# A flamingo block on one core: where bulk transfers, statistics and GpSimd's pieces stand in the attention loop

## The chip, the core and the metric

One core of a Trainium2 chip runs the whole program. The metric is the device time of one execution in microseconds. The engines are TensorE (PE, with its weight loads PEld), VectorE (DVE), ScalarE (ACT), GpSimd (POOL) and SyncE (SP), which here only issues transfers. Each engine runs its own program in order; they meet in semaphores.

## What is computed

`x` is 8 x 224 x 2048, the context 8 x 750 x 512, all float32. Cut to what matters:

```python
def attention(q, k, v, mask):          # 32 heads of 64, 8 groups of keys and values, context of 750
    scores = jnp.einsum('bsgrd,btgd->bgrst', xq, xk) / math.sqrt(64) + mask
    probs = jax.nn.softmax(scores, axis=-1)
    return jnp.einsum('bgrst,btgd->bsgrd', probs, xv)

x = x + jnp.tanh(g_xattn[0]) * attention(_layernorm(x), ctx, ctx, mask)
x = x + jnp.tanh(g_ffn[0]) * ffn(_layernorm(x), ...)    # router, top 8 of 512 slots, gate
```

## The kernel before

The first phase, the attention, lasts to about 935 us; the second, the feed-forward part, follows and is not touched. A group is one batch and one of its 8 groups of keys and values: 64 groups. Two groups make a double group (`both`, 0 to 31), four double groups a batch; `at` is `both % 4`. The 224 rows of a batch are 128 top rows (`xa`) and 96 rest rows (`xb`, three buffers), and a group has 4 + 3 = 7 units of 128 rows by 750 scores. A double group is worked off in 7 steps (`p` = 0 to 6) of two units each.

All engines loop over the steps, each with its own lead. In step i TensorE transposes the exponentials of the pair i + 1, computes the scores of the pair i + 3, and adds the value products: of pair i - 1 with the low half of the exponentials (`value_low`), of pair i with the high half (`value_high`). VectorE takes the maxima of the scores (i + 3) and adds finished groups to x (`add_part`). ScalarE takes the exponentials (i + 2, line 753) and copies the transposed ones out of PSUM (i + 1, line 749). GpSimd computes the low bfloat16 half of the copied exponentials of pair i + 1 (line 588), the main piece of its step; the exponentials have four buffers, two pairs. Beside it GpSimd splits the keys (`split_k`, line 548) and the values (`split_v`, line 553) of each group, a sixteenth of W1 in two steps of the double groups 2 to 9 (line 615), and computes the factors of the layer norm of the next batch (`root`, `factors`).

SyncE's queue is written out by hand. Keys and values have two buffers each, so a load waits until the group two before is done: `scored` counts units whose scores are computed, `valued` units whose values are added. Also on this queue: `load_top` (1 MB of x), `load_rest` (768 KB), `gather_rest` and `spread_rest` (four small transfers each, which bring the statistics of rest rows from four blocks of partitions together and back), and `spill_rest` (twelve transfers of 64 KB, which store a batch's finished rest rows).

The statistics of the next batches are computed by VectorE one piece at a time:

```python
                if p == 3:
                    for window in (2 * both, 2 * both + 1):
                        next_stats(window)
```

With `window + 5` over 8 giving batch and place, the three rest pieces of batch b + 2 stand in step 3 of the double groups at = 1 (one) and at = 2 (two), the four top pieces in those at = 3 and at = 0.

## Time and profile before

| | |
|---|---|
| median of 3 runs | 1233.67 us (1232.75 to 1234.44) |
| the profiled execution, own time | 1235.78 us |
| its span, first to last instruction | 1233.9 us |
| TensorE busy | 1094.9 us (89%) |
| ScalarE busy | 891.0 us (72%) |
| GpSimd busy | 865.7 us (70%) |
| VectorE busy | 863.5 us (70%) |
| granted TensorE clock, mean | 0.957 of 2.4 GHz |
| moved by DMA | 95.56 MB |

Busy shares are averages over both phases. A row of a timeline stands for one or several equal instructions; "idle" in brackets is the time in which the engine had nothing to do before it, and the arrow names what ended it. A granted clock of 1.00 is 2.4 GHz, 0.50 is 1.2 GHz.

### The profile page before, as it was taken

Reading aid. Unit: us, or ns where it says so; the run is one execution under the profiler, and the core shown is the slowest. Engines: PE = TensorE matmul, PEld = TensorE weight load, DVE = VectorE, ACT = ScalarE, POOL = GpSimd, SP = SyncE. Lnnn points to the kernel's source line nnn. Section 1 sums busy time; section 2 is a strip of 40 time slices with the busy share of each in tenths; the row PEclk is TensorE's granted clock in tenths of the full one; section 3 lists DMA queues with packets and bytes.
Section 4 is the critical chain, followed back from the end, with each engine's and each line's share of the span. In section 5 each row is a group of like instructions: output and inputs, shape, how many; then the busy total and the mean of one; then the engine's idle time right before and its main releaser. Section 6 shows DMA issues by size and latency. Waiting matters only on the chain.

```text
span 1233.9 us, 42837 instructions
## 1 busy us (share of the span) xinstructions
PE 1094.9 (89%) x18276; PEld 790.3 (64%) x18276; DVE 863.5 (70%) x2134; ACT 891.0 (72%) x1159; POOL 865.7 (70%) x600
## 2 busy tenths in 40 slices
PE   4878977897789878968987999989998999999998
PEld 3666766675667656746765777767775755555554
DVE  5667756785578567747775777777884499767676
ACT  3778966896689669957976898999993244465545
POOL 5779977997799679787967988998994021242333
PEclk9889988998899889988997999999998999999999
DMA  9422232123213322321142123123114700002124
GB/s 318 135 53 56 51 89 65 41 59 80 65 42 65 87 65 47 92 74 40 41 100 65 41 57 69 42 51 73 48 40 142 284 37 1 1 34 92 81 103 171
DMA packets 102588, 95.56 MB, mean 77 GB/s; under 512 B 84481, under 2 KB 85505, under 8 KB 98562
## 3 DMA queue, kind: packets, MB, share of 16 engines
q1 hardware_dynamic: 101682, 91.79, 26.5%
q8 instruction: 146, 2.39, 0.8%
q10 hardware_dynamic: 720, 1.05, 0.2%
q14 instruction: 40, 0.33, 0.1%
HBM read 71.75 MB, written 20.97 MB: 75 GB/s over the span
## 4 chain that ended last, share of the span: by engine, by line
PE 54%; POOL 14%; ACT 13%; issue 10%; DVE 4%; DMA 3%; SPq 2%; POOLq 0%; DVEq 0%; ACTq 0%
PE psum L950 11%; PE psum L1006 11%; POOL arena L588 10%; PE psum L937 9%; ACT arena L749 6%; PE psum L982 5%; ACT arena L753 4%; PE psum L970 4%; PE psum L971 4%; PE psum L1092 3%; DMA arena<-in_x_rest 2%; DVE arena L1355 2%; POOL arena L548 2%; PE psum L993 2%; PE psum L917 1%
## 5 line engine op out<-in xcount | busy, mean ns | idle before, releaser
L588 POOL TENSOR_TENSOR arena<-arena 128x1536 bf16<-128x1536 f32 x224 | 613.6, 2748 | 87.8 <-ACT arena L749 87.4
L1355 DVE CUSTOM_DVE_ANT_0 arena<-psum,arena 128x750 f32<-128x750 f32 x448 | 406.9, 937 | 192.2 <-PE psum L937 152.6
L749 ACT ACTIVATE arena<-psum 128x768 f32<-128x768 f32 x448 | 362.7, 810 | 137.8 <-PE psum L950 74.7
L753 ACT ACTIVATE arena<-arena,neg_max 128x750 f32<-128x750 f32 x448 | 409.6, 914 | 30.8 <-DVE neg_max L1355 30.8
L937 PE MATMUL psum<-arena 64*128 64x512 bf16 (+1 forms) x2688 | 271.5, 335 | 65.3 <-DVE neg_max L1355 42.2
L950 PE MATMUL psum<-ident,arena 64*128 64x64 f32 x5376 | 270.4, 234 | 53.0 <-ACT arena L749 50.6
L950 PEld LDWEIGHTS psum<-ident,arena 64*128 64x128 f32 x5376 | 215.9, 142 | 124.9 <-issue 115.5
L937 PEld LDWEIGHTS psum<-arena 64*128 64x128 bf16 x2688 | 127.2, 97 | 161.1 <-issue 57.1
L971 PE MATMUL psum<-arena 128*128 128x64 bf16 (+1 forms) x2688 | 201.6, 195 | 1.4 <-issue 1.4
L970 PE MATMUL psum<-arena 128*128 128x65 bf16 (+1 forms) x2688 | 202.6, 197 | 0.0
L971 PEld LDWEIGHTS psum<-arena 128*128 128x128 bf16 (+1 forms) x2688 | 180.6, 100 | 1.6 <-issue 1.6
L970 PEld LDWEIGHTS psum<-arena 128*128 128x128 bf16 (+1 forms) x2688 | 181.2, 99 | 0.1
L1006 PE MATMUL psum<-arena 128*128 128x512 bf16 x672 | 162.1, 385 | 0.0
L982 PE MATMUL psum<-arena 128*128 128x65 bf16 (+1 forms) x2688 | 131.9, 199 | 0.0
L548 POOL TENSOR_TENSOR arena<-arena 128x750 bf16<-128x750 f32 x64 | 92.0, 1437 | 49.4 <-DMA arena<-in_k_t 49.4
L1006 PEld LDWEIGHTS psum<-arena 128*128 128x128 bf16 x672 | 63.3, 97 | 78.7 <-issue 1.9
L982 PEld LDWEIGHTS psum<-arena 128*128 128x128 bf16 (+1 forms) x2688 | 103.3, 100 | 15.9
L736 ACT ACTIVATE arena<-psum 128x512 bf16<-128x512 f32 x56 | 33.0, 591 | 107.0 <-PE psum L993 107.0
L1290 DVE SCALAR_TENSOR_TENSOR arena<-psum,r_den,arena 128x64 f32<-128x64 f32 x448 | 97.3, 277 | 2.3
L565 POOL TENSOR_TENSOR ga<-mv_all,eps_col 128x1 f32<-128x1 f32 (+1 forms) x12 | 2.3, 190 | 97.2 <-DVE mv_all L1310 97.2
L634 POOL TENSOR_TENSOR arena<-arena 128x512 bf16<-128x512 f32 x9 | 9.4, 1040 | 82.6 <-issue 61.9
L1248 DVE CAST arena<-psum 128x512 bf16<-128x512 f32 (+1 forms) x62 | 38.7, 624 | 28.8 <-PE psum L917 28.8
(167 smaller groups left out, 1085.9 us busy)
## 6 DMA issues: line engine op xcount, KB each, us to landing
arena<-in_k_t SPq DMA_DIRECT2D x128, 187.5 KB, 3.3
arena<-in_v_rows SPq DMA_DIRECT2D x64, 192.0 KB, 3.5
out<-arena SPq DMA_DIRECT2D x10, 1024.0 KB, 3.9
arena<-in_x_top SPq DMA_DIRECT2D x8, 1024.0 KB, 6.8
arena<-in_x_rest SPq DMA_DIRECT2D x8, 768.0 KB, 4.9
spill<-arena SPq DMA_DIRECT2D x96, 64.0 KB, 2.2
arena<-spill SPq DMA_DIRECT2D x6, 1024.0 KB, 10.3
arena<-in_w_t SPq DMA_DIRECT2D x4, 1024.0 KB, 16.6
```

The lines of the kernel that those rows point to most:

```text
L548: pool.tensor_tensor(k_lo[:, g % 2, :], k_raw[:, g % 2, :], high(k_raw[:, g % 2, :]), ALU.subtract).then_inc(k_split, 1)
L588: pool.tensor_tensor(p_lo[:, slots, :], p_sb[:, slots, :], high(p_sb[:, slots, :]), ALU.subtract).then_inc(p_split, 1)
L749: act.activation(p_sb[:, n % RING, :].rearrange("p (c h q) -> p h c q", h=2, q=HALF), turned_ps, ACT.Copy).then_inc(evac_a, 1)
L753: act.activation(s_sb[:, n % RING, 0:CTX], s_sb[:, n % RING, 0:CTX], ACT.Exp, bias=neg_max[:, n % 4, :], scale=-1.0).then_inc(exped, 1)
L937: mm = pe.matmul(flat_ps[:, score_at(s) + cols.start:score_at(s) + cols.stop], q[rows, both % 2, p, :], kk, start=(term == 0), stop=(term ...
L950: mm = pe.transpose(psum[:, 4 + h, c * HALF:(c + 1) * HALF], s_sb[rows, n % RING, c * 128:(c + 1) * 128], ident[rows, rows])
L970: pe.matmul(o, hi, high(v_raw[0:rows, u, c, :]), start=(fresh and c == 0), stop=False, skip_group_check=True)
L971: pe.matmul(o[:, 0:D], hi, v_lo[0:rows, u, c, :], start=False, stop=False, skip_group_check=True)
L982: mm = pe.matmul(mix_ps[:, g % 2, at:at + D + 1], lo, high(v_raw[0:rows, g % 2, c, :]), start=False, stop=(c == NCH - 1), skip_group_check ...
L1006: mm = pe.matmul(psum[:, 2, :], h[:, j, kk, :], w, start=(k == 0 and n == 0), stop=(k == KC - 1 and n == 2))
L1290: ins = dve.scalar_tensor_tensor(xs, o[:, m, 0:D], r_den[:, m:m + 1], xs, ALU.mult, ALU.add)
L1355: dve.tensor_tensor_reduce(s_sb[:, n % RING, 0:CTX], flat_ps[:, score_at(s):score_at(s) + CTX], mask_sb[:, max(m - REP + 1, 0), :], -1.0, ...
```

## The change

Five things are moved; no computation is added or removed.

- SyncE, in each double group: the odd keys `load_k(2 * both + 3)` and the even values `load_v(2 * both + 2)` now stand ahead of spill, gather, `load_top` and `load_rest`. `load_top` moves from at = 0 to at = 1, `load_rest` and `spread_rest` from at = 1 to at = 2.
- VectorE: the rest statistics stand in steps 1 and 3 of at = 3, the top statistics in step 3 of at = 0 and at = 1 of the batch after; the merge of the rest statistics in step 6 instead of 3. The early statistics of the second phase stand in steps 1 and 5 instead of 3.
- GpSimd: `split_v` of the odd group moves from step 1 to 0, `root` from 0 to 2, `factors` from 1 to 3, the W1 (and Wq) pieces from 0 and 3 to 2 and 6.
- ScalarE: `norm_top` moves from step 4 to 6, the second `norm_rest` from step 0 to 1.

```diff
--- before.py
+++ after.py
@@ -442,24 +442,23 @@
                 if both > 0:
                     sp.wait_ge(valued, 2 * UNITS * both)
                     load_v(2 * both + 1)
+                if at == 2 and b + 1 < BATCH:
+                    spread_rest(b + 1)
+                if both + 1 < PAIRS:
+                    sp.wait_ge(scored, 2 * UNITS * (both + 1))
+                    load_k(2 * both + 3)
+                    sp.wait_ge(valued, 2 * UNITS * both + UNITS)
+                    load_v(2 * both + 2)
                 if at == 0 and b > 0:
                     spill_rest(b - 1)
                 if at == 0 and b + 1 < BATCH:
                     gather_rest(b + 1)
-                if at == 0 and b + 2 < BATCH:
+                if at == 1 and b + 2 < BATCH:
                     load_top(b + 2)
-                if both + 1 < PAIRS:
-                    sp.wait_ge(scored, 2 * UNITS * (both + 1))
-                    load_k(2 * both + 3)
-                if at == 1 and b + 1 < BATCH:
-                    spread_rest(b + 1)
-                if at == 1 and b + 2 < BATCH:
+                if at == 2 and b + 2 < BATCH:
                     if b >= 1:
                         sp.wait_ge(spilled[(b + 2) % 3], 16 * REP * NB * ((b - 1) // 3 + 1))
                     load_rest(b + 2)
-                if both + 1 < PAIRS:
-                    sp.wait_ge(valued, 2 * UNITS * both + UNITS)
-                    load_v(2 * both + 2)
 
             def load_piece(i):
                 slot = i % STAGE_SLOTS
@@ -595,7 +594,7 @@
                                        ALU.mult, ALU.add).then_inc(top_second, 1)
                 if both < 0:
                     continue
-                if p == 1:
+                if p == 0:
                     split_v(2 * both + 1)
                 if both + 1 < PAIRS:
                     if p == 1:
@@ -605,18 +604,18 @@
                     if p == 5:
                         split_v(2 * both + 2)
                 if both % 4 == 2 and both // 4 + 1 < BATCH:
-                    if p == 0:
+                    if p == 2:
                         root(both // 4 + 2, whole)
-                    if p == 1:
+                    if p == 3:
                         factors(both // 4 + 2, whole)
-                if p in (0, 3) and 2 <= both < 2 + KC // 2:
-                    n = 2 * (both - 2) + p // 3
+                if p in (2, 6) and 2 <= both < 2 + KC // 2:
+                    n = 2 * (both - 2) + p // 6
                     pool.wait_ge(w1_loaded[n // 4], 16)
                     pool.tensor_tensor(w1_lo[:, n, :], w1_raw[:, n, :], high(w1_raw[:, n, :]), ALU.subtract).then_inc(w1_split, 1)
                 if both == PAIRS - 1 and p == 5:
                     root2(0, EARLY)
-                if p in (0, 3) and both == 10:
-                    n = p // 3
+                if p in (2, 6) and both == 10:
+                    n = p // 6
                     pool.wait_ge(wq_hi_done, 1)
                     pool.tensor_tensor(wq_cat[:, 8 * n:8 * n + 8, BOT:2 * BOT], wq_raw[:, 8 * n:8 * n + 8, :], wq_cat[:, 8 * n:8 * n + 8, 0:BOT],
                                        ALU.subtract).then_inc(wq_split, 1)
@@ -765,14 +764,14 @@
                         exp_unit(2 * (i + 2) + s)
                 if i in (-2, -1):
                     round_first(i + 3)
-                if both >= 0 and p == 4 and both + 2 < PAIRS:
+                if both >= 0 and p == 6 and both + 2 < PAIRS:
                     norm_top(both + 2)
                 later = both // 4 + 1
                 if both >= 0 and both % 4 == 3 and later < BATCH:
                     if p == 0:
                         norm_rest(later, 0)
+                    if p == 1:
                         norm_rest(later, 1)
-                    if p == 1:
                         norm_rest(later, 2)
                 if both == 1 and p == 0:
                     act.wait_ge(small_loaded, 80)
@@ -1318,13 +1317,20 @@
                 dve.tensor_scalar(h_rows[:, j % 2, :], rows[:, 512 * j:512 * j + 512], mv_all[:, t, 0:1], rstd_all[:, t:t + 1],
                                   ALU.subtract, ALU.mult).then_inc(h_staged, 1)
 
-            def next_stats(window):
-                b, at = divmod(window + 5, KV)
-                b += 1
-                if window >= 3 and b < BATCH and at < NB:
-                    rest_stats(b, at)
-                elif window >= 3 and b < BATCH and at < NB + 4:
-                    top_stats(b, at - NB)
+            def next_stats(both, p):
+
+                if both == 0:
+                    for j in {0: (0, 1), 1: (2,)}.get(p, ()):
+                        rest_stats(1, j)
+                    for c in {3: (0, 1), 5: (2, 3)}.get(p, ()):
+                        top_stats(1, c)
+                b = (both - 3) // 4 + 2
+                if both < 3 or b >= BATCH:
+                    return
+                for j in {(3, 1): (0,), (3, 3): (1, 2)}.get((both % 4, p), ()):
+                    rest_stats(b, j)
+                for c in {(0, 3): (0, 1), (1, 3): (2, 3)}.get((both % 4, p), ()):
+                    top_stats(b, c)
 
             def early_stats(window):
                 u, c = divmod(window - EARLY_AT, 4)
@@ -1372,19 +1378,15 @@
                         split_q(both + 1, 0)
                     if p == 6:
                         split_q(both + 1, 1)
-                if both == 0:
-                    for j in {0: (0, 1), 1: (2,)}.get(p, ()):
-                        rest_stats(1, j)
-                    for c in {3: (0, 1), 5: (2, 3)}.get(p, ()):
-                        top_stats(1, c)
-                if p == 3 and both % 4 == 1 and both // 4 + 1 < BATCH:
-                    merge_top(both // 4 + 1)
-                    merge_rest(both // 4 + 1)
-                if p == 3:
-                    for window in (2 * both, 2 * both + 1):
-                        next_stats(window)
-                        if EARLY_AT <= window < EARLY_AT + 4 * EARLY:
-                            early_stats(window)
+                next_stats(both, p)
+                if both % 4 == 1 and both // 4 + 1 < BATCH:
+                    if p == 3:
+                        merge_top(both // 4 + 1)
+                    if p == 6:
+                        merge_rest(both // 4 + 1)
+                window = 2 * both + p // 5
+                if p in (1, 5) and EARLY_AT <= window < EARLY_AT + 4 * EARLY:
+                    early_stats(window)
                 if i == NP - 4:
                     stage_h(0, 0)
                     stage_h(0, 1)
```

On SyncE, the double groups at = 0 and at = 1 of batch 1 (both = 4 and 5) before. It begins behind the first keys and values of double group 4; `in_k_t` is a load of keys, `in_v_rows` of values:

```order
L416 DMA spill<-arena 256x1x64 x12
L404 DMA gathered<-stats_rest 32x3x6 x4
L392 DMA arena<-in_x_top 128x2048
L396 DMA arena<-in_k_t 64x750 x2
L399 DMA arena<-in_v_rows 128x6x64
L396 DMA arena<-in_k_t 64x750 x2
L399 DMA arena<-in_v_rows 128x6x64
L396 DMA arena<-in_k_t 64x750 x2
L409 DMA ln_mv<-mv_rest 32x6 x4
L389 DMA arena<-in_x_rest 128x1536
L399 DMA arena<-in_v_rows 128x6x64
```

The same engine of the changed kernel, the same batch's second to fourth place: it begins with the gathers, which follow the twelve spills at the end of a double group at = 0.

```order
L404 DMA gathered<-stats_rest 32x3x6 x4
L396 DMA arena<-in_k_t 64x750 x2
L399 DMA arena<-in_v_rows 128x6x64
L396 DMA arena<-in_k_t 64x750 x2
L399 DMA arena<-in_v_rows 128x6x64
L392 DMA arena<-in_x_top 128x2048
L396 DMA arena<-in_k_t 64x750 x2
L399 DMA arena<-in_v_rows 128x6x64
L409 DMA ln_mv<-mv_rest 32x6 x4
L396 DMA arena<-in_k_t 64x750 x2
L399 DMA arena<-in_v_rows 128x6x64
L389 DMA arena<-in_x_rest 128x1536
```

The bulk (`in_x_top`, `in_x_rest`, spill and gather) stands behind the keys and values of its double group, the spread (`ln_mv`) and `in_x_rest` one double group later.

On GpSimd, one double group with W1 pieces before, from its step 6 of the one ahead (line 588 the main piece of a step, 615 the W1 piece, 553 a value split, 548 a key split):

```order
L588 TENSOR_TENSOR arena<-arena 128x1536 x2
L615 TENSOR_TENSOR arena<-arena 128x512
L588 TENSOR_TENSOR arena<-arena 128x1536
L553 TENSOR_TENSOR arena<-arena 128x384
L548 TENSOR_TENSOR arena<-arena 128x750
L588 TENSOR_TENSOR arena<-arena 128x1536 x2
L615 TENSOR_TENSOR arena<-arena 128x512
L588 TENSOR_TENSOR arena<-arena 128x1536
L548 TENSOR_TENSOR arena<-arena 128x750
L588 TENSOR_TENSOR arena<-arena 128x1536
L553 TENSOR_TENSOR arena<-arena 128x384
L588 TENSOR_TENSOR arena<-arena 128x1536 x2
```

And in the changed kernel, where the same instructions carry line numbers one lower:

```order
L587 TENSOR_TENSOR arena<-arena 128x1536
L552 TENSOR_TENSOR arena<-arena 128x384
L587 TENSOR_TENSOR arena<-arena 128x1536
L547 TENSOR_TENSOR arena<-arena 128x750
L587 TENSOR_TENSOR arena<-arena 128x1536
L614 TENSOR_TENSOR arena<-arena 128x512
L587 TENSOR_TENSOR arena<-arena 128x1536 x2
L547 TENSOR_TENSOR arena<-arena 128x750
L587 TENSOR_TENSOR arena<-arena 128x1536
L552 TENSOR_TENSOR arena<-arena 128x384
L587 TENSOR_TENSOR arena<-arena 128x1536
L614 TENSOR_TENSOR arena<-arena 128x512
```

Before, a step had up to two pieces beside the main one, and some had none; now no step has more than one of these.

## Rows read from the trace of the kernel before

**Rows 1.** The page: two of the DMA issues (KB each, median us to landing).

```profile
arena<-in_v_rows SPq DMA_DIRECT2D x64, 192.0 KB, 3.5
...
spill<-arena SPq DMA_DIRECT2D x96, 64.0 KB, 2.2
```

**Rows 2.** The list of waits: total us, times, longest.

```profile
POOL arena L548 <- DMA arena<-in_k_t: 49.4, 9, 8.3
DVE stats_rest L1222 <- DMA arena<-in_x_rest: 45.6, 7, 8.2
```

**Rows 3.** SyncE's timeline, 140 to 480 us: start, us, what, how many.

```profile
149.67 8.72 SPq L416 DMA_DIRECT2D spill<-arena  x12
158.44 3.68 SPq L404 DMA_DIRECT2D gathered<-stats_rest  x4
162.16 0.59 SPq L392 DMA_DIRECT2D arena<-in_x_top  x1
162.79 1.46 SPq L396 DMA_DIRECT2D arena<-in_k_t  x2
...
192.57 1.06 SPq L389 DMA_DIRECT2D arena<-in_x_rest  x1
...
226.81 0.57 SPq L399 DMA_DIRECT2D arena<-in_v_rows  x1
236.78 1.11 SPq L396 DMA_DIRECT2D arena<-in_k_t  x2
...
475.62 0.60 SPq L399 DMA_DIRECT2D arena<-in_v_rows  x1
```

**Rows 4.** GpSimd's timeline; in brackets its idle time before, and the releaser.

```profile
151.59 0.83 POOL L553 TENSOR_TENSOR arena<-arena 128x384 bf16<-128x384 f32 x1
...
170.03 1.44 POOL L548 TENSOR_TENSOR arena<-arena 128x750 bf16<-128x750 f32 x1 [7.11 <-DMA arena<-in_k_t]
...
475.96 2.75 POOL L588 TENSOR_TENSOR arena<-arena 128x1536 bf16<-128x1536 f32 x1 [0.43 <-ACT arena L749]
480.46 2.75 POOL L588 TENSOR_TENSOR arena<-arena 128x1536 bf16<-128x1536 f32 x1 [1.74 <-ACT arena L749]
...
758.82 1.44 POOL L548 TENSOR_TENSOR arena<-arena 128x750 bf16<-128x750 f32 x1 [3.77 <-DMA arena<-in_k_t]
```

**Rows 5.** VectorE's timeline, double group 5, step 3.

```profile
197.81 0.69 DVE L1222 BATCH_NORM_STATS2 stats_rest<-arena 128x6 f32<-128x512 f32 x1 [7.77 <-DMA arena<-in_x_rest]
```

**Rows 6.** Stretches (columns in the first line): double 1, four pairs, doubles 6, 7, 14, 29.

```profile
core 0: us, PE busy (x) PEld busy (x) DVE busy (x) ACT busy (x) POOL busy (x), PEclk, DMA share, GB/s
55.87:88.45 32.58, 25.68 (x513) 19.84 (x510) 20.27 (x56) 24.35 (x33) 23.53 (x12) 0.90 0.23 62
142.26:207.86 65.60, 52.26 (x1014) 39.99 (x1013) 39.55 (x106) 45.50 (x58) 50.79 (x28) 0.87 0.32 78
617.70:682.49 64.79, 51.25 (x1017) 39.58 (x1016) 39.64 (x106) 45.74 (x59) 46.91 (x24) 0.89 0.32 79
735.21:788.34 53.13, 49.69 (x1024) 38.69 (x1022) 39.98 (x107) 45.99 (x59) 46.81 (x23) 0.97 0.29 62
840.57:890.65 50.08, 48.37 (x1025) 37.44 (x1022) 40.36 (x105) 45.98 (x59) 46.80 (x23) 1.00 0.29 65
207.86:236.09 28.23, 25.75 (x543) 19.84 (x541) 21.18 (x56) 24.02 (x31) 26.93 (x17) 1.00 0.18 44
236.09:261.66 25.57, 23.46 (x503) 18.25 (x501) 19.49 (x52) 24.58 (x32) 25.35 (x15) 1.00 0.20 48
446.28:472.78 26.50, 24.73 (x525) 19.17 (x521) 20.40 (x54) 23.55 (x30) 24.93 (x15) 1.00 0.20 47
867.25:890.65 23.40, 22.44 (x487) 17.78 (x487) 19.07 (x51) 22.05 (x29) 23.34 (x12) 1.00 0.21 53
```

**Rows 7.** Line 399's transfer issued at 475.62 us: time to landing.

```profile
DMA to landing us min/median/max: 3.9/3.9/3.9
```

**Rows 8.** ScalarE's timeline: a copy of turned exponentials.

```profile
485.59 0.81 ACT L749 ACTIVATE arena<-psum 128x768 f32<-128x768 f32 x1 [0.61 <-PE psum L950]
```

## The prediction, made before the changed kernel was run

> **What bounds the kernel now.** I started with the chain that ended last (its shares told little), then the list of waits, then the timelines of GpSimd and SyncE in one batch, and last a table of stretches, one per double group or pair of them. A double group (the loop variable `both`, 0 to 31) has seven steps p = 0 to 6; `at` is its place in its batch of four. The chain passes through all engines in turn, and in the first phase none is busy without a break: no engine alone is the bound, so the question is which stalls stop all of them.
>
> The list of waits names two kinds that come back once a batch [rows 2]. GpSimd's split of keys waits 49.4 us in 9 places for the key transfer, at most 8.3; VectorE's statistics of the rest rows wait 45.6 us in 7 places for x_rest, at most 8.2. SyncE's timeline says why [rows 3]. In the first double group of a batch (both = 4) the twelve spill transfers take SyncE 8.72 us to issue, the four gathers 3.68 us, then x_top goes out at 162.16, and only then, at 162.79, the keys of the odd group. GpSimd gets them at 170.03, after 7.11 us of idling [rows 4]. In the next double group x_rest is issued at 192.57, while VectorE's program already asks for it in the same step: its statistic starts at 197.81, 7.77 us idle [rows 5].
>
> The table of stretches gives the price [rows 6]. The pairs at = 0 and 1 of batches 1 to 5 (five pairs, first and last shown) last 65.6 to 64.8 us, 65.5 on average, and TensorE's granted clock in them averages 0.87 to 0.89, so part of each ran at 1.2 and not at 2.4 GHz. The doubles after them, at 1.00, last 28.2 and 25.6 us where GpSimd also splits W1 (doubles 2 to 9), and 26.5 where it does not. Double 29, with nothing extra on any engine, lasts 23.4. Where GpSimd splits W1 it is itself the bound: 25.35 us busy of 25.57. The result to forecast is the length of a pair without its two stalls.
>
> **The change part by part.**
>
> *Keys before the bulk.* Spill, gather and x_top no longer stand before the odd keys. The k wait at p = 4 goes in seven doubles (4, 8, ... 28); the other two, at the start, stay, since they wait for the first loads. The bulk is issued after the values of the next group, and the next key load follows, in an undisturbed double, 10.0 us after that value load (226.81 to 236.78) [rows 3]. x_top or x_rest (one issue of 0.6 to 1.1 us) fits into that. Spill and gather do not: 0.57 + 8.72 + 3.68 = 13.0 us, so in double at = 1 the first keys and, behind them on SyncE's queue, the odd values are issued about 3.0 us late. I call this the overrun.
>
> *x_rest and its statistics.* The load now stands at the end of double at = 2, the first statistic at p = 1 of at = 3: four steps of some 3.65 us (25.57 / 7) instead of none. The load landed 5 us after its issue (192.57 to 197.81) [rows 3, 5], so the VectorE stall goes in all six double groups at = 1 (1, 5, ... 21; the seventh place is the start). What is late next: nothing of VectorE, which gets at most two statistics (0.69 each [rows 5]) in a step, as now.
>
> *Root, factors, spread.* The spread moves behind the odd values of at = 2, root to p = 2, factors to p = 3, the ScalarE norm to p = 6. Four spread issues (the four gathers took 3.68 us [rows 3]) and a landing like the spill's 2.2 us [rows 1] lie between the merge and root, which now has more than two steps, 7 us. I cost it at nothing; if late, it stops GpSimd by 1 to 2 us in six doubles.
>
> *One piece a step on GpSimd.* The sum of its work stays; only its place changes. At p = 1 it had a main piece (the split of the exponentials) 2.75, a value split 0.83 and a key split 1.44, 5.0 us against a step of 3.6; now at most 4.2 [rows 4]. The price is the value split at p = 0: those values are issued only when TensorE has finished the last product of the group before. In double 15 they are issued at 475.62 and land 3.9 us later, 479.5 [rows 3, 7]; the main piece of p = 0 ends at 475.96 + 2.75 = 478.71 [rows 4]. So GpSimd will stand 0.8 us, split for 0.83, and start the next main piece at 480.35; today it starts at 480.46, since it waits for ScalarE. In doubles without W1 this is free. In doubles 2 to 9, where GpSimd has no idle time, what it stands comes on top, between 0 (GpSimd then lags, and its main piece of p = 0 ends later) and 0.8 each: I take 0.5.
>
> *Price of the overrun.* With values 3.0 us late, GpSimd's next main piece starts about 3 us late. How much of it the others absorb: the main piece of 480.46 ends at 483.21, and ScalarE's copy that needs its buffer starts at 485.59 [rows 4, 8], a slack of 2.4. So without W1 the loss lies between 0.5 and 3; I take 1.5, as the slack is often smaller. With W1 all 3.0 count.
>
> That the issues and not the transfers make the overrun is read from two rows: a spill transfer lands 2.2 us after its issue [rows 1], but twelve of them keep SyncE for 8.72 us [rows 3]. I keep the overrun. A rule speaks against it: the Trainium skill, page "DMA: Bandwidth & Descriptors", section "Issuing engines are not separate DMA queues", says that the time to initiate a DMA is usually small relative to the DMA itself. By that rule the block of 16 issues would hold nothing up and the forecast would be 12 us lower; the trace does not agree.
>
> *The sum.*
> - Two pairs with W1 (doubles 4, 5 and 8, 9): 65.5 to 25.6 + 25.6 + 3.0 = 54.2: 2 x 11.3 = 22.6.
> - Three pairs without (12 to 21). A plain double: pair 24, 25 lasts 53.1 with a k wait of 3.8 [rows 4, 6], so 49.3 / 2 = 24.6; the bounds are 23.4 (double 29) and 26.5 [rows 6]. 65.5 to 49.2 + 1.5: 3 x 14.8 = 44.4.
> - Pair 24, 25: 53.1 to 50.7, 2.4. Pair 28, 29: 50.1 to 24.6 + 23.4 = 48.0, 2.1 (its spill has no gather behind it).
> - Double 1: 32.6 with an x_rest stall; to about 26.2: 6.4.
> - Doubles at = 2 that follow a stall: 28.2 to 27.2 (GpSimd busy 26.93) twice, 26.5 to 26.0 four times: 4.0.
> - Values at p = 0 in doubles 2 to 9: minus 8 x 0.5 = 4.0.
>
> 22.6 + 44.4 + 4.5 + 6.4 + 4.0 - 4.0 = 77.9 us. The second phase (from 935 us on) keeps its code and its inputs. The profiled execution took 1235.8 (span 1233.9 and 1.9 around it), 2.1 above the median of 1233.67; so a profile after of about 1157.9 and a median of 1155.8, rounded to 1156. For measurement, 0.2% (2.5 us) is about what can be told from no change.
>
> **The rivals.**
>
> 1. *The bulk block costs nothing* so that the overrun term, 2 x 3.0 + 4 x 1.5 = 12 us, goes: 1144. For it: even steps on GpSimd, and value splits that never pile on key splits. Against: 13.0 us of issue in a gap of 10.0. This is also the time by the skill's rule above.
>
> 2. *The value wait at p = 0 becomes a stall of its own.* Values land 3.5 us after issue at the median [rows 1], with more in some doubles. If GpSimd's standing costs a net 1 us in 28 doubles: +28, 1184. If the overrun also brings TensorE's clock down as the old stalls did (a mean of 0.87 over 65.5 us is 17 us at 1.2 GHz, 8.5 for each of two stalls, of which I count a quarter as lost), 2 us more in six doubles: 1196. For it: a wait shorter than 1 us is all that separates double 15 from it. Against: the slack of 2.4.
>
> 3. *Slower than before.* The same place, the value split of p = 0, ahead of the main piece in GpSimd's queue; behind it the copy of ScalarE, the transposes and the value products of TensorE, whose end releases the next value load. It decides from 78 / 31 = 2.5 us net per double on; with a slack of 2.4 the values would have to land some 5 us behind the main piece and not 0.8. At 3 us: 1156 + 93 = 1249. Nothing in the landings shows it.
>
> 4. *No effect*: the stalls only change places, the spill block stopping double at = 1 as long as it stops at = 0 today, and the x_rest stall replaced by one at the spread. Then only the 4.5 us of the last two pairs stay: 1229. Against it: the lateness is 3 us and not 7, and x_rest gets four steps.
>
> **How the numbers follow.** Forecast (1148 to 1170): 0.60. Rival 1 (1138 to 1148): 0.17. Rival 2 (1170 to 1200): 0.16. Rival 4: 0.04, of which 0.02 within 0.2%. Rival 3: 0.03. The range of 8 in 10, comes from the bounds 23.4 and 26.5 of the plain double (nine doubles: 11 us down, 17 up) and of the overrun (0 to 3 us in six: 12 down, 6 up); not all of it comes together, so 1142 to 1180, the forecast's own range and the near parts of rivals 1 and 2. Faster 0.94, same 0.02, slower 0.04.
>
> **What the profile after would show.** Right: no x_rest wait on VectorE beyond the first, key waits on GpSimd only at the start; pairs at = 0 and 1 of 49 to 55 us at a clock near 1.00; in its place waits of GpSimd for in_v_rows, under 1 us in most doubles, 3 to 4 us in those of at = 1 behind a spill. Wrong: value waits above 2 us everywhere, a wait of `ln_ve` for the spread, a plain double of over 26.5 us at full clock (then ScalarE or TensorE bounds it and the stalls had hidden that), or clock falls that stay.

## The result, and the profile after

The changed kernel takes 1155.37 us (median of 4, 1153.81 to 1157.99), the kernel before 1233.21 in its runs beside it: ratio 0.9371, 95% interval 0.9351 to 0.9392. The profiled execution has a span of 1152.0 us.

Its page, the share of the chain by engine:

```profile
span 1152.0 us, 42802 instructions
...
PE 42%; POOL 29%; issue 13%; ACT 12%; DVE 2%; DMA 1%; SPq 1%; POOLq 0%; DVEq 0%; ACTq 0%
```

The chain now leans on GpSimd, 29% against 14% before. The list of waits: the lines of GpSimd that answer to [rows 2] or took their place, and ScalarE's wait for GpSimd's main piece, which was 56.5 us in 16 places before, at most 8.5 (the line numbers of GpSimd and ScalarE are one lower than before; line 552 is the value split, 547 the key split, 748 ScalarE's copy, 587 the main piece of GpSimd):

```profile
ACT arena L748 <- POOL arena L587: 42.7, 47, 3.8
POOL arena L552 <- DMA arena<-in_v_rows: 37.1, 22, 4.7
...
POOL arena L547 <- DMA arena<-in_k_t: 1.5, 1, 1.5
```

The wait of VectorE for x_rest is gone from the list, the key wait of GpSimd has one place left of nine, and GpSimd now waits 37.1 us in 22 places for values. The stretches that answer to [rows 6]: double 1, the pairs 4 and 5, 12 and 13, 16 and 17, 20 and 21, 24 and 25, 28 and 29, then the doubles 6, 7, 14, 15, and 29 alone:

```profile
core 0: us, PE busy (x) PEld busy (x) DVE busy (x) ACT busy (x) POOL busy (x), PEclk, DMA share, GB/s
51.89:77.17 25.28, 24.08 (x515) 18.59 (x513) 18.97 (x52) 24.23 (x33) 23.43 (x12) 1.00 0.31 91
129.27:183.37 54.10, 49.82 (x1028) 38.69 (x1026) 40.60 (x106) 46.29 (x60) 50.66 (x28) 0.97 0.33 80
341.51:394.18 52.67, 49.65 (x1030) 38.57 (x1026) 40.29 (x106) 46.06 (x59) 46.87 (x24) 0.97 0.34 82
444.95:499.06 54.11, 50.97 (x1030) 39.42 (x1026) 40.17 (x106) 46.09 (x59) 46.86 (x23) 0.94 0.34 80
551.10:603.05 51.95, 48.47 (x1033) 37.50 (x1029) 40.55 (x106) 46.11 (x59) 46.78 (x23) 1.00 0.35 83
654.76:707.86 53.10, 49.69 (x1028) 38.39 (x1026) 40.88 (x107) 46.05 (x59) 46.83 (x24) 0.97 0.28 62
759.35:809.21 49.86, 48.48 (x1032) 37.52 (x1028) 40.25 (x106) 46.13 (x59) 46.79 (x23) 1.00 0.30 66
183.37:211.24 27.87, 24.84 (x521) 18.97 (x517) 19.80 (x55) 23.55 (x30) 26.96 (x18) 1.00 0.28 73
211.24:236.54 25.30, 23.33 (x503) 18.36 (x505) 20.19 (x53) 24.25 (x32) 25.30 (x14) 1.00 0.19 49
394.18:420.09 25.91, 25.49 (x534) 19.36 (x529) 20.10 (x56) 24.21 (x31) 24.99 (x16) 1.00 0.29 78
420.09:444.95 24.86, 22.90 (x495) 18.11 (x497) 19.87 (x52) 23.81 (x32) 23.39 (x13) 1.00 0.20 50
784.28:809.21 24.93, 24.19 (x517) 18.70 (x515) 20.13 (x54) 23.01 (x30) 23.40 (x12) 1.00 0.26 58
```

Three things are to be seen in these rows: the clock (0.94 to 1.00 where it was 0.87 to 0.89), the pairs of 52 to 54 us where 65.5 stood, and one pair, 24 and 25, that did not get shorter at all: 53.1 before and after. SyncE in the pair 4 and 5, and GpSimd beside it:

```profile
145.29 0.57 SPq L399 DMA_DIRECT2D arena<-in_v_rows  x1
145.91 9.93 SPq L416 DMA_DIRECT2D spill<-arena  x12
155.88 2.92 SPq L404 DMA_DIRECT2D gathered<-stats_rest  x4
158.85 1.23 SPq L396 DMA_DIRECT2D arena<-in_k_t  x2
160.12 1.48 SPq L399 DMA_DIRECT2D arena<-in_v_rows  x1
```

```profile
158.28 2.76 POOL L587 TENSOR_TENSOR arena<-arena 128x1536 bf16<-128x1536 f32 x1
164.48 0.83 POOL L552 TENSOR_TENSOR arena<-arena 128x384 bf16<-128x384 f32 x1 [3.44 <-DMA arena<-in_v_rows]
165.26 2.75 POOL L587 TENSOR_TENSOR arena<-arena 128x1536 bf16<-128x1536 f32 x1
```

The even values go out at 145.29, then twelve spills (9.93 us) and four gathers (2.92), and the next keys at 158.85, 13.6 us after those values; the odd values follow at 160.12. GpSimd finishes its main piece at 161.0 and stands 3.44 us for them. The split starts when the transfer has landed, 4.4 us after its issue. How much of such a stop reaches ScalarE is seen in double 17, GpSimd's value split and the copy that follows it:

```profile
479.63 0.83 POOL L552 TENSOR_TENSOR arena<-arena 128x384 bf16<-128x384 f32 x1 [4.66 <-DMA arena<-in_v_rows]
483.26 0.81 ACT L748 ACTIVATE arena<-psum 128x768 f32<-128x768 f32 x1 [3.59 <-POOL arena L587]
```

Of 4.66 us of GpSimd's idling 3.59 us arrive at ScalarE. Doubles 13, 21 and 25 are alike: 4.39, 3.53 and 4.52 us on GpSimd, 3.33, 2.46 and 3.46 us on ScalarE, so 1.1 us is absorbed each time; in doubles 5 and 9, where GpSimd has no other idle time, all of it arrives. Of the 37.1 us of value waits 22.3 stand in the six doubles behind a spill and its gathers (5, 9, 13, 17, 21, 25).

### The profile page after: what moved, and what is told of

It reads as the page before. It is cut to its first block, busy times and chain, and to the rows that moved or that the text cites. A ratio compares the mean times of both kernels' runs of the same rounds, so it can differ in the third digit from the quotient of the medians.

```text
span 1152.0 us, 42802 instructions
## 1 busy us (share of the span) xinstructions
PE 1071.3 (93%) x18241; PEld 775.3 (67%) x18276; DVE 864.8 (75%) x2134; ACT 891.2 (77%) x1159; POOL 865.2 (75%) x600
## 4 chain that ended last, share of the span: by engine, by line
PE 42%; POOL 29%; issue 13%; ACT 12%; DVE 2%; DMA 1%; SPq 1%; POOLq 0%; DVEq 0%; ACTq 0%
POOL arena L587 20%; PE psum L1005 12%; PE psum L949 7%; ACT arena L748 7%; PE psum L936 5%; POOL arena L547 4%; ACT arena L752 4%; PE psum L981 3%; PE psum L1091 3%; PE psum L969 2%; PE psum L970 2%; PE psum L992 2%; POOL arena L614 1%; ACT arena L723 1%; PE psum L1130 1%
## 5 line engine op out<-in xcount | busy, mean ns | idle before, releaser
L748 ACT ACTIVATE arena<-psum 128x768 f32<-128x768 f32 x448 | 363.4, 811 | 82.6 <-POOL arena L587 42.7
L949 PE MATMUL psum<-ident,arena 64*128 64x64 f32 x5376 | 265.6, 231 | 53.4 <-ACT arena L748 49.4
L949 PEld LDWEIGHTS psum<-ident,arena 64*128 64x128 f32 x5376 | 210.9, 140 | 125.9 <-issue 116.9
L936 PE MATMUL psum<-arena 64*128 64x512 bf16 (+1 forms) x2688 | 262.3, 327 | 3.8 <-DVE neg_max L1361 2.2
L970 PE MATMUL psum<-arena 128*128 128x64 bf16 (+1 forms) x2688 | 198.0, 194 | 1.4 <-issue 1.4
L969 PE MATMUL psum<-arena 128*128 128x65 bf16 (+1 forms) x2688 | 198.8, 195 | 0.1
L936 PEld LDWEIGHTS psum<-arena 64*128 64x128 bf16 x2688 | 124.4, 95 | 93.7 <-issue 9.4
L970 PEld LDWEIGHTS psum<-arena 128*128 128x128 bf16 (+1 forms) x2688 | 176.9, 99 | 1.7 <-issue 1.7
L969 PEld LDWEIGHTS psum<-arena 128*128 128x128 bf16 (+1 forms) x2688 | 177.4, 98 | 0.1
L1005 PE MATMUL psum<-arena 128*128 128x512 bf16 x654 | 158.2, 384 | 1.5 <-issue 0.3
L981 PE MATMUL psum<-arena 128*128 128x65 bf16 (+1 forms) x2688 | 129.0, 197 | 0.0
L981 PEld LDWEIGHTS psum<-arena 128*128 128x128 bf16 (+1 forms) x2688 | 100.8, 98 | 15.4
L552 POOL TENSOR_TENSOR arena<-arena 128x384 bf16<-128x384 f32 x64 | 53.0, 829 | 37.1 <-DMA arena<-in_v_rows 37.1
```

The lines of the kernel that those rows point to most:

```text
L748: act.activation(p_sb[:, n % RING, :].rearrange("p (c h q) -> p h c q", h=2, q=HALF), turned_ps, ACT.Copy).then_inc(evac_a, 1)
L936: mm = pe.matmul(flat_ps[:, score_at(s) + cols.start:score_at(s) + cols.stop], q[rows, both % 2, p, :], kk, start=(term == 0), stop=(term ...
L949: mm = pe.transpose(psum[:, 4 + h, c * HALF:(c + 1) * HALF], s_sb[rows, n % RING, c * 128:(c + 1) * 128], ident[rows, rows])
L969: pe.matmul(o, hi, high(v_raw[0:rows, u, c, :]), start=(fresh and c == 0), stop=False, skip_group_check=True)
L970: pe.matmul(o[:, 0:D], hi, v_lo[0:rows, u, c, :], start=False, stop=False, skip_group_check=True)
L981: mm = pe.matmul(mix_ps[:, g % 2, at:at + D + 1], lo, high(v_raw[0:rows, g % 2, c, :]), start=False, stop=(c == NCH - 1), skip_group_check ...
```

## The experiments

Eleven kernels were timed. Ratios are against the kernel before, in the same series.

**The value split back in step 1.**

```diff
                     continue
-                if p == 0:
+                if p == 1:
                     split_v(2 * both + 1)
```

> The changed kernel with one move undone: GpSimd splits the odd group's values in step 1 again, not in step 0. My theory (the late issue of the values behind spill and gather costs time because GpSimd stands at step 0): the value waits of 37.1 us go nearly all, the six doubles at = 1 lose their excess of some 3 us each (28.79, 27.07, 28.30, 29.75, 26.98, 28.39 against 24.9 to 25.3 beside them, 19 us in all), and a step with two pieces costs about 0.5 us in some 20 doubles: 1146 us, between 1140 and 1152. Rival (the even steps are worth more than the value wait costs): 1156 or more.

Measured: 1133.08 us, ratio 0.9209 (0.9170 to 0.9247), 22 us below the changed kernel, more than expected. The value waits:

```profile
POOL arena L552 <- DMA arena<-in_v_rows: 3.0, 4, 1.1
```

37.1 us have become 3.0. The move of the value split from step 1 to step 0, which was part of the change, cost time: one step more of cover hides values that are issued 3 us late. The step that again holds two pieces costs nothing that shows: plain doubles last 24.37 us here too.

**The spill in two halves.**

```diff
 
-            def spill_rest(b):
+            def spill_rest(b, blocks=range(REP)):
                 sp.wait_ge(x_added, KV * (b + 1))
-                for r in range(REP):
+                for r in blocks:
                     for j in range(NB):
...
                     load_v(2 * both + 2)
-                if at == 0 and b > 0:
-                    spill_rest(b - 1)
                 if at == 0 and b + 1 < BATCH:
                     gather_rest(b + 1)
+                if at in (0, 1) and b > 0:
+                    spill_rest(b - 1, range(2 * at, 2 * at + 2))
                 if at == 1 and b + 2 < BATCH:
```

> The changed kernel with the spill in two halves: gather and six spill transfers behind the double group at = 0, the other six behind at = 1. Same instructions, no block of over 7.5 us on SyncE. If the overrun is what GpSimd waits for behind a spill, the long value waits (3.4, 1.7, 4.4, 4.7, 3.5, 4.5) shrink to the 1.5 us of plain doubles and the time falls by 14 to 20 us, to about 1138. Rival (the values land late because of traffic or a late product, not because of the queue): no change, 1153 to 1158.

Measured: 1135.74 us, ratio 0.9222 (0.9190 to 0.9253), 20 us below the changed kernel. SyncE at the place shown above, and the value waits:

```profile
146.57 0.57 SPq L399 DMA_DIRECT2D arena<-in_v_rows  x1
147.19 3.37 SPq L404 DMA_DIRECT2D gathered<-stats_rest  x4
150.60 4.82 SPq L416 DMA_DIRECT2D spill<-arena  x6
156.44 1.17 SPq L396 DMA_DIRECT2D arena<-in_k_t  x2
157.65 0.60 SPq L399 DMA_DIRECT2D arena<-in_v_rows  x1
```

```profile
POOL arena L552 <- DMA arena<-in_v_rows: 20.3, 20, 1.9
```

The keys now follow the even values after 9.9 us, as in a double without bulk, and of the waits 20.3 us are left, none over 1.9. So the queue, not traffic, made the values late by those 3 to 4 us: the same bytes were moved. The clock stays at 1.00 in all pairs here.

**Both together.** The two edits above in one kernel, nothing else.

> Both repairs together: spill in halves and the value split in step 1. If the two repairs remove the same wait from its two ends, only what each leaves over is gained: 1.1 + 0.8 + 0.9 us of value waits and their echo in doubles 13, 14, 17, 25: 1129 to 1132, within 0.3% of the better one alone. Rival (they add up, 22 + 20): 1113.

Measured: 1129.76 us over 5 runs, ratio 0.9156 (0.9139 to 0.9174), the shortest time with that of the next experiment. The two repairs remove the same wait from its two ends: 22 and 20 us alone, 26 together. With the spill in halves, moving the split back still gains 6 us (1135.74 to 1129.76): that is what the value waits outside the overrun cost. The other 16 of the 22 us are the overrun's. Doubles 4, 17 and 19 in it:

```profile
131.62:156.92 25.30, 24.48 (x517) 18.86 (x515) 20.38 (x53) 23.29 (x31) 25.30 (x14) 1.00 0.30 65
461.86:486.23 24.37, 24.20 (x519) 18.73 (x516) 20.19 (x54) 23.01 (x30) 23.44 (x13) 1.00 0.41 93
512.32:537.17 24.85, 22.89 (x495) 18.06 (x497) 19.86 (x52) 23.80 (x32) 23.43 (x12) 1.00 0.20 50
```

With W1 GpSimd is busy for all of 25.30 us; without it TensorE for 24.20 of 24.37 us at 2.4 GHz. In these doubles GpSimd waits for no transfer, and every plain double of this kernel, 29 too, has 24.37 us. So the 23.4 us that double 29 took before [rows 6] was never the length of a plain double: the one ahead of it took 26.7, with a wait of GpSimd for keys of 1.92 us, and behind that wait GpSimd worked without a break (23.34 us busy of 23.40) and made up for it. The two together, 50.1 us, are longer than two of 24.37. Doubles at = 2 without W1, which also hold root and factors, last 26.1 us.

**The W1 pieces back in steps 0 and 3,** on top of both repairs:

```diff
                         factors(both // 4 + 2, whole)
-                if p in (2, 6) and 2 <= both < 2 + KC // 2:
-                    n = 2 * (both - 2) + p // 6
+                if p in (0, 3) and 2 <= both < 2 + KC // 2:
+                    n = 2 * (both - 2) + p // 3
                     pool.wait_ge(w1_loaded[n // 4], 16)
```

> The kernel with both repairs, and the W1 and Wq pieces back in steps 0 and 3; with the value split in step 1 that is GpSimd's uneven order of before, but for root and factors. Theory (GpSimd is busy without a break in doubles 2 to 9, so places there change nothing, as long as none of them waits): no change, 1127 to 1132. Rival (one piece a step is itself worth time): 2 us or more slower in doubles 2 to 10, 1133 or more.

Measured: 1128.80 us, ratio 0.9145 (0.9125 to 0.9164): not to be told from the 0.9156 above. The edit moves the pieces of W1 alone; those of Wq in double 10, which the expectation names too, stayed in steps 2 and 6. One piece a step is by itself worth nothing here.

**Bulk ahead of the odd keys again.**

```diff
                     spread_rest(b + 1)
+                if at == 0 and b > 0:
+                    spill_rest(b - 1)
+                if at == 0 and b + 1 < BATCH:
+                    gather_rest(b + 1)
+                if at == 0 and b + 2 < BATCH:
+                    load_top(b + 2)
                 if both + 1 < PAIRS:
...
                     load_v(2 * both + 2)
-                if at == 0 and b > 0:
-                    spill_rest(b - 1)
-                if at == 0 and b + 1 < BATCH:
-                    gather_rest(b + 1)
-                if at == 1 and b + 2 < BATCH:
-                    load_top(b + 2)
                 if at == 2 and b + 2 < BATCH:
```

> The changed kernel with spill, gather and x_top ahead of the odd keys of at = 0 again; x_rest, statistics and GpSimd's places stay new. Theory (keys first is worth the stall of 7 to 8 us less the overrun it makes): key waits of 7 to 8 us in doubles 4 to 20, 3.8 and 1.9 later (some 44 us), value waits behind a spill gone (19 us): about 1155 + 46 - 19 = 1182. Rival (the overrun eats most of what keys first gives): 1155 to 1165.

Measured: 1175.33 us, ratio 0.9542 (0.9508 to 0.9576), 20 us above the changed kernel. The waits:

```profile
POOL arena L547 <- DMA arena<-in_k_t: 42.7, 9, 8.3
...
POOL arena L552 <- DMA arena<-in_v_rows: 14.5, 17, 1.6
```

42.7 us of key waits are back in the nine places of before and 22.6 us of the value waits are gone. So keys first is worth 20 us net of the value waits it makes, somewhat less than the 27 expected. (`load_top` went back with spill and gather, and has no share of its own in this number.)

**x_rest and its statistics as before.**

```diff
                     load_k(2 * both + 3)
+                if at == 1 and b + 2 < BATCH:
+                    if b >= 1:
+                        sp.wait_ge(spilled[(b + 2) % 3], 16 * REP * NB * ((b - 1) // 3 + 1))
+                    load_rest(b + 2)
+                if both + 1 < PAIRS:
                     sp.wait_ge(valued, 2 * UNITS * both + UNITS)
...
                     load_top(b + 2)
-                if at == 2 and b + 2 < BATCH:
-                    if b >= 1:
-                        sp.wait_ge(spilled[(b + 2) % 3], 16 * REP * NB * ((b - 1) // 3 + 1))
-                    load_rest(b + 2)
 
...
 
-            def next_stats(both, p):
-
-                if both == 0:
-                    for j in {0: (0, 1), 1: (2,)}.get(p, ()):
-                        rest_stats(1, j)
-                    for c in {3: (0, 1), 5: (2, 3)}.get(p, ()):
-                        top_stats(1, c)
-                b = (both - 3) // 4 + 2
-                if both < 3 or b >= BATCH:
-                    return
-                for j in {(3, 1): (0,), (3, 3): (1, 2)}.get((both % 4, p), ()):
-                    rest_stats(b, j)
-                for c in {(0, 3): (0, 1), (1, 3): (2, 3)}.get((both % 4, p), ()):
-                    top_stats(b, c)
+            def next_stats(window):
+                b, at = divmod(window + 5, KV)
+                b += 1
+                if window >= 3 and b < BATCH and at < NB:
+                    rest_stats(b, at)
+                elif window >= 3 and b < BATCH and at < NB + 4:
+                    top_stats(b, at - NB)
 
...
                         split_q(both + 1, 1)
-                next_stats(both, p)
-                if both % 4 == 1 and both // 4 + 1 < BATCH:
-                    if p == 3:
-                        merge_top(both // 4 + 1)
-                    if p == 6:
-                        merge_rest(both // 4 + 1)
-                window = 2 * both + p // 5
-                if p in (1, 5) and EARLY_AT <= window < EARLY_AT + 4 * EARLY:
-                    early_stats(window)
+                if both == 0:
+                    for j in {0: (0, 1), 1: (2,)}.get(p, ()):
+                        rest_stats(1, j)
+                    for c in {3: (0, 1), 5: (2, 3)}.get(p, ()):
+                        top_stats(1, c)
+                if p == 3 and both % 4 == 1 and both // 4 + 1 < BATCH:
+                    merge_top(both // 4 + 1)
+                    merge_rest(both // 4 + 1)
+                if p == 3:
+                    for window in (2 * both, 2 * both + 1):
+                        next_stats(window)
+                        if EARLY_AT <= window < EARLY_AT + 4 * EARLY:
+                            early_stats(window)
                 if i == NP - 4:
```

> The changed kernel with x_rest issued in at = 1 between odd keys and even values, and VectorE's statistics and merges in the steps of before; all else new. Theory: the x_rest stall of 7 to 8 us comes back in six doubles, with the fall of TensorE's clock: 1155 + 6 x 7.5 = 1200, a little less where it hides the overrun in the same double (1185 to 1200). Rival (the x_rest wait was covered by the key stall's backlog): below 1170.

Measured: 1160.68 us (1156.56 to 1169.11), ratio 0.9413 (0.9369 to 0.9456), an interval that overlaps that of the changed kernel. The expectation of 1200 fell. Waits for x_rest, then VectorE's first statistic and SyncE's issues in double 5:

```profile
DVE stats_rest L1222 <- DMA arena<-in_x_rest: 11.5, 6, 4.8
```

```profile
180.51 0.69 DVE L1222 BATCH_NORM_STATS2 stats_rest<-arena 128x6 f32<-128x512 f32 x1 [1.45 <-DMA arena<-in_x_rest]
```

```profile
174.22 1.11 SPq L396 DMA_DIRECT2D arena<-in_k_t  x2
175.38 0.58 SPq L389 DMA_DIRECT2D arena<-in_x_rest  x1
```

x_rest is asked for in the same step in which it is issued, as before, and yet the waits come to 11.5 us, not 45.6. What had stood between the keys and x_rest before was the spread, which in this kernel is still in at = 2. I formed a second theory from this: the spread in front made the load late.

That is only half of it. The overrun stops the same doubles, and it hides a part of the wait for x_rest. In double 5 VectorE comes late to its own statistic, held up by TensorE, and in double 1, which has no overrun, the wait is the 4.8 us of the list:

```profile
177.59 0.94 DVE L1355 CUSTOM_DVE_ANT_0 arena<-psum,arena 128x750 f32<-128x750 f32 x1 [2.41 <-PE psum L950]
73.49 0.69 DVE L1222 BATCH_NORM_STATS2 stats_rest<-arena 128x6 f32<-128x512 f32 x1 [4.76 <-DMA arena<-in_x_rest]
```

In double 1 VectorE is at the statistic 1.2 us after the issue of x_rest, in doubles 5, 9, 13, 17 and 21 3.2 to 4.6 us after it. Double 1 lasts 30.85 us in this kernel and 25.28 in the changed one, 5.6 us more where the two medians differ by 5.3. So this experiment doesn't show that a use in the step of the issue is cheap; it says that behind the overrun it costs little more. The shares of the single doubles can't be told closer, since the profiled execution is the slowest of the four, 1169.11 us.

**And the spread ahead of x_rest again,** on top of the last one:

```diff
                     load_v(2 * both + 1)
-                if at == 2 and b + 1 < BATCH:
-                    spread_rest(b + 1)
                 if both + 1 < PAIRS:
...
                     load_k(2 * both + 3)
+                if at == 1 and b + 1 < BATCH:
+                    spread_rest(b + 1)
                 if at == 1 and b + 2 < BATCH:
```

> The kernel that kept x_rest and its statistics as before (1160.7 us), and the spread ahead of x_rest on SyncE again, as before the change. There the x_rest waits fell to 11.5 us from 45.6. Theory: it was the spread in front (its wait for the merge in the same step, and four issues of 2.5 to 3.7 us) that made x_rest late by 4 to 5 us. Then the x_rest waits return to some 40 us and the time rises by 6 x 5 = 30 to about 1190. Rival (the key stall a double earlier made it late): no change, 1155 to 1165.

Measured: 1201.07 us, ratio 0.9724 (0.9698 to 0.9750): 40 us more for the place of four transfers of 0.8 KB.

```profile
174.37 1.11 SPq L396 DMA_DIRECT2D arena<-in_k_t  x2
179.36 2.47 SPq L409 DMA_DIRECT2D ln_mv<-mv_rest  x4
181.88 0.58 SPq L389 DMA_DIRECT2D arena<-in_x_rest  x1
```

```profile
DVE stats_rest L1222 <- DMA arena<-in_x_rest: 46.0, 6, 9.0
```

After the keys at 174.37 SyncE waits for VectorE's merge until 179.36, issues the spread in 2.47 us, and x_rest leaves at 181.88, 7.5 us behind the keys instead of 1.2. VectorE meanwhile stands in front of the statistic. The rival, the key stall, is ruled out: this kernel waits for keys once, at the start, for 1.5 us. The merge itself comes late here because of the overrun: in the kernel before, the spread starts 2.4 us behind the keys, and x_rest 4.9 us behind them.

**The kernel before, with x_rest ahead of the spread.**

```diff
                     load_k(2 * both + 3)
-                if at == 1 and b + 1 < BATCH:
-                    spread_rest(b + 1)
                 if at == 1 and b + 2 < BATCH:
...
                     load_rest(b + 2)
+                if at == 1 and b + 1 < BATCH:
+                    spread_rest(b + 1)
                 if both + 1 < PAIRS:
```

> The kernel before, with one exchange on SyncE: x_rest ahead of the spread. By the same theory the x_rest waits fall from 45.6 to below 20 us and the time by 6 x 4 = 24 us or a little more, with the clock's fall: 1205 to 1212. Rival: no change, 1230 to 1236.

Measured: 1213.82 us, ratio 0.9836 (0.9809 to 0.9863), 19 us faster than before by one exchange, less than the 24 expected. The x_rest waits fall from 45.6 to 28.5 us, not below 20:

```profile
DVE stats_rest L1222 <- DMA arena<-in_x_rest: 28.5, 6, 6.0
```

The 28.5 us that remain are the use in the step of the issue: in all six doubles VectorE is at the statistic 1.2 us after the issue of x_rest, which takes 4.9 to 7.2 us from its issue to the start of the statistic. In the kernel with the new key order VectorE came later, and 11.5 us remained.

**ScalarE's norms.** Doubles at = 3 without W1 lasted 26.2 us before and last 24.86 now, which I had not forecast. Three kernels looked for the cause. First the second rest norm back in step 0, on the kernel of the first experiment:

```diff
                         norm_rest(later, 0)
+                        norm_rest(later, 1)
                     if p == 1:
-                        norm_rest(later, 1)
                         norm_rest(later, 2)
```

> The kernel of the value split in step 1 (1133 us), and the second of ScalarE's three norms of rest rows back in step 0 of at = 3. Doubles at = 3 last 24.84 us there and lasted 26.2 before the change. If the norm's place is the cause, the five doubles at = 3 without W1 and after return to 26.2: 1133 + 5 x 1.35 = 1140. Rival (VectorE's statistics, which left step 3, are the cause): no change, 1131 to 1135.

Measured: 1133.23 us, ratio 0.9186 (0.9172 to 0.9200): no change from 0.9209; its expectation fell. Nor are VectorE's statistics the cause: the kernel with x_rest and its statistics as before has them in the old steps, and its doubles at = 3 last 24.84 to 24.86 us. Then the top norm, on the kernel with both repairs:

```diff
                     round_first(i + 3)
-                if both >= 0 and p == 6 and both + 2 < PAIRS:
+                if both >= 0 and p == 4 and both + 2 < PAIRS:
                     norm_top(both + 2)
```

> The kernel with both repairs (1129.8 us), and ScalarE's norm of top rows in step 4 again instead of 6. Doubles at = 3 last 24.85 us there and lasted 26.2 before the change; neither the rest norm nor the statistics explain it. If this norm does: doubles at = 3 of 26.2 and plain ones a few tenths longer, 5 x 1.35 + 9 x 0.3 = 9 us, 1139. Rival (GpSimd's places are the cause): no change, 1127 to 1132.

Measured: 1146.10 us, ratio 0.9279 (0.9256 to 0.9303), 16 us more. The norm's wait for GpSimd's factors, and doubles 17, 18 and 19:

```profile
ACT arena L723 <- POOL ln_bias L541: 15.2, 8, 3.9
```

```profile
471.89:496.62 24.73, 24.20 (x514) 18.73 (x512) 20.27 (x53) 23.01 (x30) 23.43 (x13) 1.00 0.42 90
496.62:523.07 26.45, 24.73 (x524) 19.09 (x524) 19.41 (x54) 23.40 (x30) 24.98 (x16) 1.00 0.37 101
523.07:548.84 25.77, 23.66 (x507) 18.36 (x503) 20.53 (x53) 24.60 (x32) 23.47 (x13) 1.00 0.20 48
```

This mixed two things, the place and a wait for the factors that now come in step 3. So the same with at = 2 left in step 6:

```diff
                     round_first(i + 3)
-                if both >= 0 and p == 6 and both + 2 < PAIRS:
+                if both >= 0 and p == (6 if both % 4 == 2 else 4) and both + 2 < PAIRS:
                     norm_top(both + 2)
```

> The kernel with both repairs, ScalarE's norm of top rows in step 4 in the double groups at = 0, 1 and 3 alone; at = 2 keeps step 6, so that it never waits for GpSimd's factors. With the norm in step 4 everywhere the time was 1146.1 us: plain doubles 24.73 instead of 24.37, those at = 3 25.8 to 26.7 instead of 24.85, and 11 us of waits for the factors. If the place itself costs: plain 24.73, at = 3 about 26.2, in all 17 x 0.36 + 7 x 1 = 13 us, 1142. If the wait for the factors was most of it: 1133 to 1137.

Measured: 1134.89 us, ratio 0.9206 (0.9190 to 0.9223), 5 us above the kernel with both repairs. Doubles 17, 18 and 19:

```profile
464.01:488.74 24.73, 24.20 (x514) 18.73 (x512) 20.28 (x53) 23.01 (x30) 23.43 (x13) 1.00 0.40 90
488.74:515.17 26.43, 25.93 (x538) 19.65 (x536) 20.33 (x56) 24.04 (x31) 24.97 (x16) 1.00 0.34 98
515.17:540.01 24.84, 22.43 (x487) 17.77 (x487) 19.71 (x51) 23.93 (x32) 23.42 (x12) 1.00 0.20 50
```

The plain double has 24.73 us in both (24.37 with the norm in step 6): 0.36 us for the place. The double at = 3 is at 24.84 here, though its own norm stands in step 4. It is longer only where the norm of at = 2 stands in step 4: 25.8 us in doubles 19 and 27, and 26.7 in the other batches, in each of which the clock fell to 1.2 GHz for 3.4 us in or behind the double at = 2. What was late in at = 2 is paid in at = 3. Of the 16 us 11 go with the norm of at = 2, and its wait for the factors is in them.

## Why the prediction was right, and where only its sum was

The forecast was 1156, the measurement 1155.37. Point by point, in its own order:

- *Keys before the bulk*: right. The seven key waits are gone.
- *The overrun*: the mechanism was right (keys 13.6 us after the even values, forecast 13.0), the size too small. I had 3 us in doubles with W1 and 1.5 in those without, 12 us in all. Halving the spill gave 20 us. The step that was mis-sized is "a slack of 2.4", read from one place: it was 1.1 us in all four doubles without W1, and the stop of GpSimd was 3.5 to 4.7 us, not 3.0. So the three pairs without W1 lasted 52.7, 54.1 and 52.0, not 50.7. In two of the three the clock also fell, to a mean of 0.97 and 0.94. The halved spill also refutes rival 1, the block that costs nothing. The Trainium skill ("DMA: Bandwidth & Descriptors", section "Issuing engines are not separate DMA queues") says that the time to initiate a DMA is usually small beside the DMA itself, and by that rival 1 would have been right. Here 16 issues one behind another took 12.85 us, and the measurement decides against the rule.
- *Pair 24 and 25*: forecast 2.4 us shorter, measured 0. The key wait of 3.8 us was traded for a value wait of 4.5.
- *The value wait at p = 0*: I gave it 0.5 us in doubles 2 to 9 and nothing in the plain ones. It was the other way round: outside the overrun GpSimd waited 1.1 us in all in doubles 2 to 9, and 1.2 to 1.5 us in each of doubles 20, 24 and 28 to 30. "In doubles without W1 this is free" was the wrong step: one double that was just in time stood for all. Its price is the 6 us between the halved spill alone and both repairs; most of the 22 us from moving the split back is the overrun's.
- *Double 29*: the 23.4 us that the sum takes for it, and that the range takes as the lower bound of a plain double, is a double that made up for the one before, as shown above. A plain double takes 24.37. With its value wait of 1.5 us double 29 took 24.9.
- *x_rest*: its stall went, as forecast, and the reason given is one of two. The prediction blamed that "VectorE's program already asks for it in the same step", and counted steps of cover. In the kernel before, that is the larger part: 28.5 of 45.6 us of waits remain when x_rest goes ahead of the spread. The other part, 17 us of waits and 19 us of time, is the spread ahead of it on SyncE's queue, which waited for VectorE's merge in that step. In the new order the merge comes later and the spread counts for more, 40 of the 45.7 us between the kernel with rest and spread as before and the changed one. The row of its issue stood between the keys and x_rest in the order before, and I costed only its new place ("at nothing") and not the old one. No kernel moved the statistics alone, so whether the four steps of cover would have been enough with the spread in its old place is open.
- *Root, factors, spread at their new places*: no wait for them is in the trace; right.
- *Doubles at = 3 and at = 2*: without W1, those at = 3 were left at 26.2 and measured 24.86. This is a gain that I had not seen. It goes with the top norm in step 6, and by the last three experiments with that of at = 2 above all. Those at = 2 were taken as 26.0, half a us shorter than before; they took 25.9 to 27.2, 26.6 on average, and got no shorter at all. The value wait of p = 0 is in them.
- *Double 1*: 26.2 forecast, 25.3 measured. The start of the loop, which I took as unchanged, took 25.6 us in double 0 in this execution and 29.8 before, but anything from 25.6 to 29.1 in the experiments that leave its loads as they are in the changed kernel; nothing is concluded from it.

So the figure fits better than its parts, and that is luck. In the two profiles the first phase lost 81.5 us where the sum had 77.9 (1153.81 against 1157.9 us). Less was gained than forecast in the pairs without W1 (7.2 us), in 24 and 25 (2.3), in 28 and 29 (1.9) and in the four doubles at = 2 without W1 (3.0), 14.4 together. More was gained in doubles 2 to 10 (7.6, of which 4.0 had been taken off for value waits that hardly came), in the doubles at = 3 from 11 on (5.5), in double 1 (0.9) and in double 0 (4.2), 18.2 together.

## What to carry to other kernels

On a queue that issues in order, list for each transfer what stands ahead of it and what that waits for: four transfers of 0.8 KB that wait for a merge cost 19 us in the kernel before, and 40 in another order, by standing ahead of a load, and sixteen issues in a block filled 13 us of a gap of 10, where in two parts they fitted. Place the use of a freshly loaded tile by the latest landing over all loops, not by one that was just in time. Take the length of an undisturbed stretch from several of them, and not from one that follows a stall: it may be catching up. An experiment that puts one stall back beside another can show it too cheap, as the first stop hides the second. And an even filling of an engine that never waits gained nothing.

## What the runs showed of the hardware that was not expected

The issues cost SyncE time by their number and not by their bytes: the load of x_rest, 768 KB, took it 0.58 us above, twelve spills of 64 KB, 768 KB as well, 8.3 to 9.9 us in the changed kernel. Six spills took 4.82 us, 0.80 each, twelve with four gathers 12.85 us, 0.80 each again, though one lands after 2.2 us [rows 1]. Where the spills stood decided on 20 us with the same bytes moved.

TensorE's clock went down to 1.2 GHz also after the shorter stalls, for 3.4 to 6.8 us: in doubles 5, 13, 17 and 25, where TensorE stood idle for 3.17, 2.73, 2.75 and 2.85 us just before the fall or while it came. In double 21, after 1.86 us of idling, it stayed at 2.4 GHz, and in the doubles of 24.37 us it stood at 1.00.
